# Loading x in 512-byte runs and turning it on VectorE in a quantized feed-forward kernel

## The chip, the cores and the metric
One NeuronCore of a Trainium2 chip runs the whole kernel. The metric is the device time of one execution in microseconds, the median of several.

## What is computed
`x` is (4, 1024, 512) float32, `cond_512` (4, 256). A relation is formed from x, its mean over the sequence and the condition, and goes through a feed-forward part with activations quantized to uint8 steps and weights to int8 steps; the result is added to x:

```python
fused = concatenate([x, x_mean * ones_L, hidden[:, None, :] * ones_L], axis=-1)   # hidden = [cond, cond]
relation = relu(einsum('bld,do->blo', fused, W) + b)          # W (1536, 512)
h = relu(quant_linear(relation, w1, b1))                       # w1 (2048, 512)
out = x + quant_linear(h, w2, b2)                              # w2 (512, 2048)
# quant_linear: s = max(x)/255, xq = clip(round(x/s), 0, 255)*s; each weight row by max|w|/127; bias to s_in*s_w
```

The scale of the activations is the maximum over the whole tensor, so no activation can be quantized before every relation is known.

## The kernel before
The 4096 rows of x are eight blocks n = 0..7 of 512 rows. Five instruction streams are written out by hand and joined by semaphores: SP issues the DMAs, PE is TensorE, ACT ScalarE, DVE VectorE, POOL GpSimd.

**Phase 1, the relation.** The contraction over the depth (512, in KD = 4 chunks of 128) needs x with the depth on the partitions. A block arrives in `x_in` with four consecutive rows of x in each partition (runs of 8 KB; block 0 in two halves with runs of 4 KB, L219). `turn_x` (L332) turns it on TensorE: 16 transposes of 128x128 into the four PSUM banks `XT[k]` (L337; for block 0 L367). ScalarE copies each bank, rounded to float32r, into `x_hi` (`take_hi`, L511) and sums it for the mean; VectorE puts the rest into `x_lo` (`take_lo`, L632). The weight is split in the same manner into `cw_hi` (L543) and `cw_lo` (L670). `relation(n, par, ot)` (L341 to L351) forms one of four tiles of 128 output columns as 12 products of 512 columns, x_hi cw_hi + x_lo cw_hi + x_hi cw_lo for each chunk, in one of two banks `REL`; a tile's bank is free again when `take_relation` (L635, VectorE) has copied it to `raw` with its maximum, which is why `relation` waits for `rel_taken`, two tiles back.

Beside it the weights of the feed-forward part are quantized, one chunk of 1 MB per block: VectorE finds the row maxima (`scale_w`, L642 to L654), ScalarE rounds (L519), VectorE casts (`cast_w`, L659), TensorE transposes (`turn_w`, L353 to L360, 16 transposes), ScalarE copies out (L526, L533).

The order on each engine in block n (x two blocks deep, `par` the buffer): TensorE relation 0, `turn_x(n + 1)`, relations 1 to 3, `turn_w(n)`. VectorE (`phase1_block`, L690): `take_relation(n, 0)`, `scale_w(n)`, `take_lo(n + 1)` for chunks 0 to 2, `take_relation(n, 1)`, `take_lo` for chunk 3, `take_relation(n, 2)`, `cast_w(n)`, `take_relation(n, 3)`. ScalarE: `take_hi(n + 1)`, the rounding of the weights, the copies out. SP: when `x_turned` shows that block n has been read out of x_in, x of block n + 2; when the weights of n have been rounded, the weights of n + 2; after the first two of these, `cw_rest` (the other 1024 rows of W, 2 MB, L247) and `b2_b` (L248). Ahead of block 0 TensorE runs products on the identity (`keep_warm`, L330). Small rows (condition, biases) are turned on TensorE after block 0's x (L375 to L377) and copied by VectorE (L681 to L688).

**Phases 2 and 3.** `product1` (L443) forms the hidden activations, `take_h` (L784) copies them with their maxima, half of them go to DRAM and back; `product2` (L473) forms the output, `finish` (L836) scales it, adds x (`x_res`, loaded again at L270 and L297, 8 KB per partition) and SP stores it (L286, L305).

## Time and profile before

| | us |
|---|---|
| three runs | 355.8, 356.89, 454.16 |
| median | 356.89 |
| span of the profiled execution, first to last instruction | 353.6 |
| TensorE busy in it | 346.3 |
| VectorE busy | 270.5 |
| ScalarE busy | 170.7 |

The profile is of one execution, whose own time is its span; what lies around the span is the difference to the runs. In the rows, PE is TensorE's products, PEld its weight loads, SPq the queue of SP. The names of tensors are those that share the memory: `bank` is PSUM, `hidden` is also `raw`, `pool_r` also cw_in, cw_rest and the weight steps, `pool_q` the raw feed-forward weights. The chain of waits is the work that ended last, followed back; in it and in the timelines a product's end is modelled.

### The profile page before, as it was taken

How to read it: one execution, taken by the hardware profiler on the slowest of the kernel's cores; microseconds unless marked ns; L12 is line 12 of the kernel's file. 1: busy time of each engine (PE TensorE's matmuls, PEld its weight loads, DVE VectorE, ACT ScalarE, POOL GpSimd, SP SyncE). 2: the span in 40 equal slices, each digit the busy share in tenths (PEclk: the TensorE clock that was granted, in tenths of full speed). 3: DMA queues.
4: the chain of work that ended last, by engine and by line, in shares of the span. 5: the costliest groups of instructions: out<-in, count | busy, mean ns of one | idle time of the engine just before them, and what ended most of it. 6: DMA issues, size and time to landing. Idle time of an engine off the chain costs nothing.

```text
span 353.6 us, 5697 instructions
## 1 busy us (share of the span) xinstructions
PE 346.3 (98%) x1774; PEld 202.6 (57%) x1774; DVE 270.5 (77%) x588; ACT 170.7 (48%) x285; POOL 1.1 (0%) x8
## 2 busy tenths in 40 slices
PE   6899999999999999999999999999999999999996
PEld 6688888888887744444444444444444444444444
DVE  1867567576485579999999999988495685785996
ACT  3655546447345299991000000009959569578800
POOL 1000000000000000000000000000000000000000
PEclk9999999999999999999999999999999999999999
DMA  7961981641300007887785030026986279977416
GB/s 265 399 255 43 339 336 59 237 154 83 120 0 2 0 1 294 346 342 326 311 297 224 0 119 0 0 78 244 387 362 237 120 284 424 399 222 222 167 63 237
DMA packets 13295, 70.72 MB, mean 200 GB/s; under 512 B 1224, under 2 KB 1504, under 8 KB 5856
## 3 DMA queue, kind: packets, MB, share of 16 engines
q1 hardware_dynamic: 13280, 70.54, 51.6%
q8 instruction: 8, 0.13, 0.2%
q14 instruction: 7, 0.06, 0.0%
HBM read 45.37 MB, written 25.17 MB: 199 GB/s over the span
## 4 chain that ended last, share of the span: by engine, by line
PE 92%; issue 3%; DVE 3%; DMA 1%; ACT 0%; DVEq 0%
PE bank L480 27%; PE bank L446 26%; PE bank L349 24%; PE bank L501 4%; PE bank L337 3%; PE bank L456 2%; PE bank L359 2%; PE bank L330 1%; DMA x_in<-in_x_dram 1%; DVE hidden L792 1%; PE bank L367 1%; DVE x_lo L632 1%; PE bank L401 1%; PE bank L435 0%; DVE cw_lo L670 0%
## 5 line engine op out<-in xcount | busy, mean ns | idle before, releaser
L592 ACT ACTIVATE steps<-hidden,s_quant 128x512 int16 (+1 forms) x124 | 76.8, 708 | 98.8 <-DVE s_quant L815 78.2
L446 PE MATMUL bank<-pool_r,w_t 128*128 (+1 forms) x480 | 103.8, 379 | 0.0
L792 DVE TENSOR_SCALAR_CACHE_REDUCE hidden<-bank,qb,hmax 128x512 f32 x128 | 97.6, 810 | 6.2 <-PE bank L456 2.3
L446 PEld LDWEIGHTS bank<-pool_r,w_t 128*128 128x128 bf16 x480 | 47.0, 98 | 56.6
L480 PE MATMUL bank<-w_t 128*128 128x512 bf16 x256 | 55.9, 379 | 0.0
L349 PE MATMUL bank<-x_hi,cw_hi 128*128 128x512 f32 x128 | 51.6, 403 | 0.9 <-issue 0.5
L349 PE MATMUL bank<-x_hi,cw_lo 128*128 128x512 f32 x128 | 50.0, 391 | 0.0
L349 PE MATMUL bank<-x_lo,cw_hi 128*128 128x512 f32 x128 | 49.9, 390 | 0.0
L637 DVE TENSOR_SCALAR_CACHE_REDUCE hidden<-bank 128x512 f32 (+1 forms) x32 | 22.0, 689 | 36.1 <-PE bank L349 36.1
L480 PEld LDWEIGHTS bank<-w_t 128*128 128x128 bf16 x256 | 25.0, 98 | 30.2 <-issue 0.2
L480 PE MATMUL bank<-w_t,pool_q 128*128 128x512 bf16 x192 | 41.9, 379 | 0.0
L480 PEld LDWEIGHTS bank<-w_t,pool_q 128*128 128x128 bf16 x192 | 18.8, 98 | 22.6
L349 PEld LDWEIGHTS bank<-x_hi,cw_hi 128*128 128x128 f32 x128 | 24.0, 188 | 7.0 <-issue 1.5
L349 PEld LDWEIGHTS bank<-x_hi,cw_lo 128*128 128x128 f32 x128 | 24.0, 188 | 5.2
L349 PEld LDWEIGHTS bank<-x_lo,cw_hi 128*128 128x128 f32 x128 | 24.1, 188 | 4.5
L511 ACT ACTIVATE x_hi<-bank 128x512 fp32r<-128x512 f32 x32 | 18.7, 598 | 13.7 <-PE bank L337 12.5
L519 ACT ACTIVATE pool_r<-pool_q,winv 128x512 int8<-128x512 f32 x32 | 20.5, 711 | 5.6 <-DVE winv L654 5.6
L632 DVE TENSOR_TENSOR x_lo<-bank,x_hi 128x512 fp32r<-128x512 f32 x32 | 20.6, 682 | 1.1 <-ACT x_hi L511 1.1
L574 ACT ACTIVATE steps<-hidden,bias_inv,s_in_inv 128x512 uint8 (+1 forms) x28 | 20.5, 802 | 1.2 <-ACT pool_r L579 1.2
L823 DVE TENSOR_SCALAR pool_q<-steps 128x2048 bf16<-128x2048 int16 x16 | 10.7, 690 | 13.0 <-ACT steps L592 12.6
L823 DVE TENSOR_SCALAR w_t<-steps 128x2048 bf16<-128x2048 int16 x15 | 10.1, 691 | 12.9 <-ACT steps L592 12.5
L533 ACT ACTIVATE w_t<-bank 128x1024 bf16<-128x1024 bf16 x8 | 7.8, 1020 | 22.7 <-PE bank L359 22.7
(104 smaller groups left out, 268.3 us busy)
## 6 DMA issues: line engine op xcount, KB each, us to landing
hidden_spill<-hidden SPq DMA_DIRECT2D x16, 1024.0 KB, 3.9
hidden<-hidden_spill SPq DMA_DIRECT2D x16, 1024.0 KB, 8.3
pool_q<-in_L_ffn_w_dram SPq DMA_DIRECT2D x8, 1024.0 KB, 5.1
pool_r<-in_x_dram SPq DMA_DIRECT2D x8, 1024.0 KB, 5.7
x_in<-in_x_dram SPq DMA_DIRECT2D x7, 1024.0 KB, 7.1
out_dram<-pool_r SPq DMA_DIRECT2D x7, 1024.0 KB, 6.0
pool_r<-in_L_cond_W_dram SPq DMA_DIRECT2D x1, 2048.0 KB, 10.9
x_in<-in_x_dram SPq DMA_DIRECT2D x2, 512.0 KB, 5.1
```

The lines of the kernel that those rows point to most:

```text
L349: mm = pe.matmul(REL[ot % 2][:, :], w[:, k, ot * P:(ot + 1) * P], v[:, par, k, :], start=(k == 0 and m == 0), stop=(k == KD - 1 and m == 2))
L446: mm = pe.matmul(bank[ft % BANKS][:, :], w1_t[:, k, ft * P:(ft + 1) * P], act_q[:, bass.ds(n * (KD * TB) + k * TB, TB)], start=(k == 0), s ...
L480: mm = pe.matmul(bank[TJ * par + j][:, :], hid_q[par][:, ft, j * P:(j + 1) * P], w2_t[:, ft, :], start=(ft == 0), stop=(ft == FT - 1))
L501: mm = pe.matmul(y_bank[:, cols], hid_q[1][:, ft, j * P:(j + 1) * P], w2_t[:, ft, cols], start=(ft == 0), stop=(ft == FT - 1))
L511: act.activation(x_hi[:, par, k, :], XT[k][:, :], ACT.Copy, accum_out=xsum[:, bass.ds(n * KD + k, 1)]).then_inc(hi_ready, 1)
L519: act.activation(w_steps[:, j * D:(j + 1) * D], w_in[:, par, j * D:(j + 1) * D], ACT.Copy, scale=winv[:, par, s:s + 1]).then_inc(w_steps_r ...
L574: ins = act.activation(act_steps[:, k * TB:(k + 1) * TB], raw[:, bass.ds((n * KD + k) * TB, TB)], ACT.Identity, scale=s_in_inv[:, 0:1], bi ...
L592: ins = act.activation(steps[:, q % 2, f, :], hidden[:, bass.ds(slot * HB + ft * TB, TB)], ACT.Copy, scale=s_quant[:, ft:ft + 1])
L632: dve.tensor_tensor(x_lo[:, par, k, :], XT[k][:, :], x_hi[:, par, k, :].bitcast(F32), ALU.subtract).then_inc(lo_ready, 1)
L637: dve.tensor_scalar(raw[:, bass.ds((n * KD + ot) * TB, TB)], REL[ot % 2][:, :], 1.0, None, ALU.mult, ALU.max, accum_out=raw_max[:, bass.ds ...
L792: dve.tensor_scalar(hidden[:, bass.ds(slot * HB + ft * TB, TB)], bank[ft % BANKS][:, :], qb1[:, ft:ft + 1], hmax[:, ft:ft + 1], ALU.add, A ...
L823: dve.tensor_scalar(hid_q[par][:, 4 * q:4 * q + 4, :], steps[:, q % 2, :, :], 0.0, 255.0, ALU.max, ALU.min).then_inc(hid_ready, 1)
```

## The change
A partition group c (32 partitions) now receives columns 128c to 128c + 127 of x: row 32q + i of the block goes to partition 32c + i, at place q, in runs of 512 bytes, by four DMAs of 32 partitions. VectorE turns each chunk k with one `dve.transpose` of 128x512 (16 squares of 32x32 per group) straight into `XT[k]`. The depth that comes to partition 32c + r of chunk k is 128c + 32k + r, so the weight is loaded in the same order (`cw_turned`), the first 512 rows by eight DMAs on ACT's queue, the next 512 by four on SP's. Block 0's relation runs chunk by chunk of the depth over four banks (`relation_by_depth`), so that it can start with the first chunk. Relations 0 and 1 of block 1 come ahead of `turn_w(0)`, and the small rows are turned behind them. The residual x and the output now go in runs of 2 KB, with row 128j + p in partition p.

```diff
+    R = 32; CG = P // R; TQ = TB // R
+    x_blocks  = ... .rearrange("(n j p) d -> n p j d", p=P, j=TJ)        # was "(n p j) d -> n p (j d)"; out_blocks alike
+    x_squares = ... .rearrange("(n q i) (c e) -> n c i q e", q=TQ, i=R, c=CG)
+    cw_turned = cond_w.rearrange("(g c k r) o -> g c r k o", c=CG, k=KD, r=R)
 # SP
             def load_x(n, par):
-                sp.dma_start(x_in[:, par, :, :]..., x_blocks[...]).then_inc(x_landed[par], 16)
+                for c in range(CG):
+                    sp.dma_start(x_in[c * R:(c + 1) * R, par, :].rearrange("i (q e) -> i q e", q=TQ),
+                                 x_squares[bass.ds(n, 1), c, :, :, :]...).then_inc(x_landed[par], 16)
-            load_half(0, x0_landed); load_cw(range(KD // 2)); load_half(1, x_landed[0])
+            load_x(0, 0)
 ...
-            load_cw(range(KD // 2, KD))
             load_x(1, 1)
 ...
-            sp.dma_start(cw_rest, cw_rows[:, KD:3 * KD, :]).then_inc(rest_landed, 16)
+            for c in range(CG):
+                sp.dma_start(cw_rest[c * R:(c + 1) * R, 0:KD, :], cw_turned[1, c]).then_inc(rest_landed, 16)
+            sp.dma_start(cw_rest[:, KD:KC, :], cw_rows[:, 2 * KD:3 * KD, :]).then_inc(rest_landed, 16)
 # TensorE
-            def turn_x(n, it, par): ...                    # and block 0's transposes
+            def relation_by_depth():
+                for k in range(KD):
+                    pe.wait_ge(lo_ready, k + 1)
+                    pe.wait_ge(cw_lo_ready, k + 1)
+                    for ot in range(KD):
+                        for m, (w, v) in enumerate(((cw_hi, x_hi), (cw_hi, x_lo), (cw_lo, x_hi))):
+                            mm = pe.matmul(bank[4 + ot][:, :], w[:, k, ot * P:(ot + 1) * P], v[:, 0, k, :], ...)
+                        if k == KD - 1:
+                            mm.then_inc(rel_done, 1)
+            keep_warm(50, ident_bf[:, :], REL[0])          # was 20 and 9
+            relation_by_depth()
+            for ot in range(2):
+                relation(1, 1, ot, taken=ot + 1)
+            turn_columns()                                 # waits rows_landed, rel_taken >= KD
+            turn_w(0, 0); turn_w(0, 1)
+            for ot in range(2, KD):
+                relation(1, 1, ot)
+            turn_w(1, 0); turn_w(1, 1)
                 # blocks 2 to 6: relations 0 to 3, turn_w
 # ACT
+            for h in range(2):
+                for c in range(CG):
+                    act.dma_start(cw_in[c * R:(c + 1) * R, ks, :], cw_turned[0, c, :, ks, :]).then_inc(cw_landed[h], 16)
             def take_cw(k):
-                act.wait_ge(cw_landed[k], 16)
+                act.wait_ge(cw_landed[k // 2], 16 * CG)
 # VectorE
+            def turn_x(n, it, par, chunks=range(KD)):
+                dve.wait_ge(x_landed[par], 16 * CG * (it + 1))
+                squares = x_in[:, par, :].rearrange("p (q k r) -> p k q r", q=TQ, k=KD)
+                for k in chunks:
+                    if n > 0:
+                        dve.wait_ge(lo_ready, KD * (n - 1) + k + 1)
+                    dve.transpose(XT[k][:, :].rearrange("p (q i) -> p q i", i=R), squares[:, k, :, :]
+                                  ).then_inc(x_turned, 1)
-            for k in range(KD // 2): take_cw_lo(k)
-            take_lo(0, 0, range(KD // 2))
-            for k in range(KD // 2, KD): take_cw_lo(k); take_lo(0, 0, [k])
+            turn_x(0, 0, 0, [0, 1])
+            for k in range(KD):
+                take_cw_lo(k)
+                take_lo(0, 0, [k])
+                if k + 2 < KD:
+                    turn_x(0, 0, 0, [k + 2])
             def phase1_block(...):
+                elif first:                                # block 0
+                    turn_x(1, 0, 1)
+                    scale_w(n, it, par, w2_rows)
+                    take_lo(1, 1, range(KD - 1))
+                    take_relation(0, 0)
                 else:
+                    turn_x(n + 1, it + par, 1 - par)
                     take_relation(n, 0)
+                    if columns:                            # block 1
+                        take_columns()
                     scale_w(n, it, par, w2_rows)
                     take_lo(n + 1, 1 - par, range(KD - 1))
-            with dve.Fori(0, KD // 2) as it: ...
+            for n in range(KD): phase1_block(n, n // 2, n % 2, False, False, first=(n == 0), columns=(n == 1))
```

## Rows read from the trace of the kernel before

**Rows 1.** The page: busy time of each engine (us, share, instructions).
```profile
PE 346.3 (98%) x1774; PEld 202.6 (57%) x1774; DVE 270.5 (77%) x588; ACT 170.7 (48%) x285; POOL 1.1 (0%) x8
```

**Rows 2.** Chain of waits in order of time: start us, us, what.
```profile
24.78 2.82 PE bank L349 x12
27.61 1.75 PE bank L337 x16
29.35 8.18 PE bank L349 x36
37.53 0.91 PE bank L359 x16
38.44 2.82 PE bank L349 x12
...
120.75 0.71 DVE hidden L637 x2
```

**Rows 3.** Stages: length; busy us of PE, PEld, DVE, ACT, POOL; clock, DMA, GB/s.
```profile
0.00:2.00 2.00, 0.09 (x2) 0.09 (x3) 0.32 (x3) 1.13 (x1) 1.09 (x8) 1.00 0.08 25
2.00:5.00 3.00, 2.22 (x20) 1.96 (x20) 0.00 (x0) 0.16 (x1) 0.00 (x0) 1.00 0.92 231
5.00:7.00 2.00, 1.82 (x9) 1.76 (x10) 0.27 (x1) 0.96 (x2) 0.00 (x0) 1.00 1.02 395
7.00:9.00 2.00, 2.00 (x18) 1.70 (x16) 1.09 (x2) 0.81 (x3) 0.00 (x0) 1.00 1.08 426
...
38.24:51.90 13.66, 13.66 (x85) 11.50 (x82) 8.88 (x18) 7.04 (x17) 0.00 (x0) 1.00 0.89 332
```

**Rows 4.** Timeline of VectorE, block 2: start us, us, what, [idle before it].
```profile
41.47 0.69 DVE L637 TENSOR_SCALAR_CACHE_REDUCE hidden<-bank 128x512 f32 x1 [3.04 <-PE bank L349]
...
42.09 2.28 DVE L646 TENSOR_REDUCE wmax<-pool_q 128x4 f32<-128x2048 f32 x1
...
44.87 1.89 DVE L632 TENSOR_TENSOR x_lo<-bank,x_hi 128x512 fp32r<-128x512 f32 x3
46.67 0.68 DVE L637 TENSOR_SCALAR_CACHE_REDUCE hidden<-bank 128x512 f32 x1
...
47.28 0.69 DVE L632 TENSOR_TENSOR x_lo<-bank,x_hi 128x512 fp32r<-128x512 f32 x1
```

**Rows 5.** Timeline of the start, TensorE, ACT and VectorE in turn; last, line L763.
```profile
1.91 2.31 PE L330 MATMUL bank<-ident_bf 128*128 128x128 bf16 x20 [1.91 <-POOL ident_bf L318]
...
5.99 1.31 ACT L543 ACTIVATE cw_hi<-pool_r 128x512 fp32r<-128x512 f32 x2 [3.83 <-DMA pool_r<-in_L_cond_W_dram]
...
10.41 0.68 DVE L670 TENSOR_TENSOR cw_lo<-pool_r,cw_hi 128x512 fp32r<-128x512 f32 x1
...
12.81 0.17 DVE L681 TENSOR_REDUCE fold<-ident 128x4 f32<-128x16 f32 x1
...
13.81 0.17 DVE L688 COPY b_col<-bank 128x16 f32<-128x16 f32 x1
...
L763 DVE TENSOR_SCALAR pool_r<-steps x4: 294/294/295, 123.9 to 126.4; 128x512 bf16<-128x512 int16 x4
```

**Rows 6.** Busy time by stretch at the end of the run, columns as in rows 3.
```profile
350.00:351.00 1.00, 0.30 (x3) 0.02 (x1) 0.63 (x2) 0.00 (x0) 0.00 (x0) 1.00 0.93 272
...
352.00:353.00 1.00, 0.00 (x0) 0.00 (x0) 0.00 (x0) 0.00 (x0) 0.00 (x0) 0.90 0.37 131
353.00:353.60 0.60, 0.00 (x0) 0.00 (x0) 0.00 (x0) 0.00 (x0) 0.00 (x0) 0.50 0.00 0
```

**Rows 7.** SP timeline, x_in issues; DMA issues with median us to landing.
```profile
20.75 0.50 SPq L202 DMA_DIRECT2D x_in<-in_x_dram  x1
...
35.85 0.56 SPq L202 DMA_DIRECT2D x_in<-in_x_dram  x1
...
pool_q<-in_L_ffn_w_dram SPq DMA_DIRECT2D x8, 1024.0 KB, 5.1
...
x_in<-in_x_dram SPq DMA_DIRECT2D x7, 1024.0 KB, 7.1
```

More of the change, by code:

```diff
@@ L330, in keep_warm, with relation @@
                     pe.matmul(free_bank[:, 0:moving.shape[-1]], ident_bf[:, :], moving, start=True, stop=True)
-            def turn_x(n, it, par):
-                pe.wait_ge(x_landed[par], 16 * (it + 1))
-                for k in range(KD):
-                    pe.wait_ge(lo_ready, KD * (n - 1) + k + 1)
-                    for j in range(TJ):
-                        mm = pe.transpose(XT[k][:, j * P:(j + 1) * P], x_in[:, par, j, k * P:(k + 1) * P],
-                                          ident[:, :])
-                    mm.then_inc(x_turned, 1)
-            def relation(n, par, ot):
-                pe.wait_ge(rel_taken, KD * n + ot + 1)
+            def relation(n, par, ot, taken=None):
+                pe.wait_ge(rel_taken, KD * n + ot - 1 if taken is None else taken)
                 for k in range(KD):
@@ L379, in _ @@
+            keep_warm(50, ident_bf[:, :], REL[0])
[3 more added lines that the diff above has]
+            turn_columns()
+            for half in range(2):
+                turn_w(0, half)
+            for ot in range(2, KD):
+                relation(1, 1, ot)
+            for half in range(2):
+                turn_w(1, half)
+            with pe.Fori(1, NB // 2 - 1) as it:
                 for par in range(2):
                     n = 2 * it + par
-                    relation(n, par, 0)
@@ L382, in _ @@
-                    turn_x(n + 1, it + par, 1 - par)
-                    for ot in range(1, KD):
+                    for ot in range(KD):
                         relation(n, par, ot)
@@ L388, in _ @@
             n = NB - 2
-            relation(n, 0, 0)
-            turn_x(n + 1, NB // 2 - 1, 1)
-            for ot in range(1, KD):
+            for ot in range(KD):
                 relation(n, 0, ot)
@@ L733, in _ @@
             by_batch = raw_max[:, :].rearrange("p (b h k) -> p h b k", h=2, k=KD)
-            with dve.Fori(0, KD // 2) as it:
-                for par in range(2):
-                    phase1_block(2 * it + par, it, par, False, False)
+            for n in range(KD):
+                phase1_block(n, n // 2, n % 2, False, False, first=(n == 0), columns=(n == 1))
             for n in range(KD, NB - 1):
```

124 lines of the change are left out of this document (53 added, 71 removed).

## The prediction

> **What bounds the kernel now.** I read the busy shares first. TensorE is busy for 346.3 of 353.6 us, VectorE for 270.5 [rows 1], so a microsecond is gained only where TensorE stops working, and VectorE isn't free either. Next the chain of waits in order of time [rows 2]: after the first 15 us it is TensorE alone through the first phase, and each 512-row block repeats four pieces: 36 products of the relation (8.18 us, so 0.227 us a product), 16 transposes of weights (0.91), 12 products (2.82), 16 transposes of x on L337 (1.75). From 24.78 to 38.44 is one block: 13.66 us. The last relation is taken at 120.75; the two later phases begin from there and hold none of the changed instructions except transfers. The table by stage then shows the room [rows 3]: in one such block VectorE works 8.88 of 13.66 us. Its own timeline [rows 4] shows where the room lies: one idle stretch of 3.04 us ahead of `take_relation(n, 0)`; between `take_relation(n, 0)` at 41.47 and the end of `take_relation(n, 1)` at 47.28 there is none.
>
> **What goes from TensorE.** Seven groups of 16 transposes (L337) of 1.75 us, 12.3 us, and those of block 0 (L367). If nothing took their place, six blocks would give 10 us and more.
>
> **What comes to VectorE.** 32 `dve.transpose` of 128x512 float32 in 16 squares each, SBUF to PSUM. No row shows one. From below: a 128x512 operation that only clips and converts, 0.29 us (L763). From above: each of the 16 squares paid like the smallest copy, 0.17 us (L688), 16 x 0.17 = 2.7 us [rows 5]. The nearest rows are the subtractions of the same size and type, which start 0.60 us apart when nothing holds them (four from 10.41 to 12.81) [rows 5]. I take 0.61, since a transpose reads and writes as many elements. Call it T.
>
> **Steady blocks (2 to 6).** Four T's stand between `take_relation(n-1, 3)` and `take_relation(n, 0)`, in the gap of 3.04 us [rows 4]. VectorE waits there for the transposes of weights and the first 12 products, and not for the x transposes, which came behind these; so the gap stays, and 4 x 0.61 = 2.44 us fit. They fit up to T = 0.77. What shows up is another wait. The fourth relation of a block may not start before `take_relation(n, 1)` has freed its bank. In the old order TensorE had 1.75 us of x transposes plus two relations (2 x 12 x 0.227 = 5.45 us) between the first and the fourth; now it has 5.45 alone. VectorE needs, from the end of the first relation (38.44 + 2.82 = 41.26 [rows 2]), 0.21 until it starts, 5.81 until 47.28, and some 0.08 for the semaphore: 6.10, against a start of the fourth at 5.45 less 0.16 (a product's end is modelled that much after its slot) = 5.29. So TensorE stalls 0.8 us per block. A block costs 13.66 - 1.75 + 0.80 = 12.7 us. Five blocks gain 5 x 0.95 = 4.75 us.
>
> **Start.** Here VectorE becomes the bound. x(0) now needs all 1 MB (four transfers) before the first transpose, with 1 MB of the weight on ACT's queue beside it. The old rates were 25 GB/s to 2 us, 231 to 5, 395 to 7, 426 to 9 [rows 3]; 2.1 MB are through at 8.4. The first cw_hi started at 5.99 [rows 5], 0.8 us after its bytes (0.79 MB into the queue) by these rates: so x(0) at 9.2 if runs of 512 bytes move as those of 4 KB. No row has such runs; if they move at half the rate (one row already shows 231 instead of 395), 11.9; if x goes ahead of the weight, 7. I take 10.0.
>
> From there VectorE has, without a pause, up to the release of relation (1, 3): 12 transposes (x(0), x(1), x(2)) 7.3 us; 15 subtractions (cw_lo 4, x_lo 4+4+3) at 0.60, 9.0; six relations taken at 0.62 (46.67 to 47.28), 3.7; two `scale_w` at 2.78 (42.09 to 44.87), 5.6; one cast 1.1; `take_columns` 1.2 (12.81 to 13.98) [rows 4, 5]. Sum 27.9 us, so the fourth relation of block 1 starts at 38.0 and the transposes of W(1) at 38.0 + 2.73 + 0.16 = 40.9. Before they stood at 37.53 [rows 2]. The start loses 3.4 us, though the relation of block 0 by depth keeps TensorE fed from the first chunk (first product about 12.6, last about 23.5): it stands still some 1.6 us ahead of block 1 and some 3 us ahead of relation (1, 3).
>
> **The clock.** TensorE now has a gap, from the end of 50 warm products (20 took 2.31 us [rows 5], so 1.9 + 5.8 = 7.7) to 12.6. At the end of the run the granted clock is 1.00 until 352, with the last products at 350.3, 0.90 in the next microsecond and 0.50 (1.2 GHz) behind it [rows 6]. So I expect the first products of block 0 at 1.2 GHz. Cover: relation (0, 0) ends some 2.5 us before VectorE comes to take it, so a loss up to 2.5 us costs nothing. The Trainium skill ("TensorE: Matmul & The Clock Gate", part 1) says that an idle array falls to half clock; the trace agrees, and with the cover the sum is the same unless the low clock stays, the rival below.
>
> **Transfers.** Later x loads are issued two blocks ahead (20.75, 35.85) and take a median of 7.1 us [rows 7]; four issues in place of one cost SP some 1.2 us (0.50 to 0.56 for one [rows 7], less where little waits), behind which only the next load waits. ACT now issues eight loads of the weight first, 8 x 0.45 = 3.6 us, and x_hi isn't wanted before 10.6: hidden. The tight one is x(4): it stands in SP's queue behind w(3), the 2 MB of cw_rest and b2 (it was issued at 35.85 before [rows 7]). w(3) now waits until about 41; 4.5 MB at 395 GB/s are 11.3 us, plus 0.9, so x(4) lands at about 54.2 and VectorE wants it at 54.7. VectorE waits in `turn_x`, and behind it stand `take_relation(3, 0)`, then `scale_w`, so TensorE would follow. I add 0.6 us for what that may miss (bounds 0 and 3). The stores and residual loads in runs of 2 KB instead of 8 KB (phase 3) have the w1 loads as a pattern: 5.1 us per 1 MB with 2 KB and 8 KB rows together [rows 7]; chunks are needed tens of microseconds after issue: nothing. The unrolled loops of VectorE: nothing, or a few tenths.
>
> **Sum.** +3.4 - 4.75 + 0.6 = -0.75 us: a span of 352.9. Of the three runs 454.16 lies far off and is left aside; 355.8 and 356.89 lie 2.2 to 3.3 above the profiled span of 353.6. That makes 355.1 to 356.2; I say 355.7. A measurement of this kernel tells about 2% (7.1 us) from no change.
>
> **Rivals.**
> *A, chance 0.59:* the above. Its bounds: T 0.55 to 0.75, x(0) at 8 to 12: -3.5 to +3, so 353 to 359.5.
> *B, the transposes cost more than the gap hides (slower), 0.15.* Each T above 0.61 costs 12 times its excess in the start, and above 0.77 also 4 x 5 times in the blocks, after which VectorE bounds the phase. T = 1.0: 4.7 + 4.6 - 0.75 = +8.5, 364; T = 1.2: 7.1 + 8.6 - 0.75 = +15, 371. 2% is passed from T = 0.95. For it: 16 separate squares, float32, a destination in PSUM; no row shows any of them. Against: three operations of 512 float32 elements (subtraction, taking a relation, a quarter of the reduction of 2048 in 2.28 us) all cost 0.57 to 0.62 in a row [rows 4, 5].
> *C, the loads at half rate, 0.13.* x(0) comes at 11.9, +1.9; one MB at half of 395 GB/s costs 2.65 us more, so x(4) comes 2.1 us after it is wanted, 1.5 more than I have added: +3.4 in all, 359.1. If the weight's loads on 32 partitions halve too, 1.3 to 2.65 more: up to 362. The Trainium skill ("SBUF — State Buffer", the DMA port swizzle) says that 32 partitions reach only 8 of the 16 ports, and ("DMA: Bandwidth & Descriptors", rules for authors) that splitting over partitions brings nothing; no row of before has a bulk load of 32 partitions, so whether it holds here is open. By that rule the result is C's.
> *D, faster by over 2%, 0.06.* T near 0.3 (-3.8 in the start) and x(0) at 7 (-3), beside my -0.75: -7.5, 349. Only the start can give this much; the stall of 0.8 per block remains whatever T is. Against: both ends needed at once.
> *E, the low clock stays through block 0, 0.07.* 48 products at 0.45: +10.9 less 2.5 covered: +8.4, 364. Against: once it runs, TensorE has 12 products per chunk without a pause.
>
> Numbers: faster 0.07 (D and a trace of A), slower 0.18 (B's larger part and E), the same 0.75. The range 351 to 362 leaves out B and E's larger part above and D below.
>
> **What would show it.** Right: `dve.transpose` at 0.60 to 0.70; blocks 2 to 6 at 12.7 us, with TensorE idle 0.8 us in each ahead of the fourth relation, released by `take_relation(n, 1)`; VectorE without idle time from x(0)'s landing to about 40 us; W(1) at about 41. Wrong: a transpose over 0.8 us; blocks of 11.9 us (no stall); VectorE waiting for x_in in any block; a clock of 0.50 beyond the first chunk; phases 2 and 3 longer than before.

## The result and the profile after

The changed kernel is slower: four runs from 363.68 to 365.58 us, median 364.46. The four runs of the kernel before are 355.53, 355.8, 356.89 and 454.16 (median 356.35); the last lies far off, and the ratio, 1.0242 with a 95% interval of 1.0213 to 1.0272, is taken without it. The profiled execution took 363.68 us with a span of 361.9 us, so the span has grown by 8.3 us, where the prediction had it shrink by 0.75. All of it lies in phase 1: from the last relation taken to the end of the span it was 232.85 us before (353.6 less 120.75 [rows 2]) and is 232.67 after (361.9 less 129.23).

The page of the kernel after, with what answers to [rows 1]; the row of L645 is the new transpose on VectorE (count | busy us, mean ns of one | idle us ahead of it):

```profile
span 361.9 us, 5473 instructions
PE 337.2 (93%) x1645; PEld 192.7 (53%) x1667; DVE 288.7 (80%) x620; ACT 170.2 (47%) x285; POOL 1.1 (0%) x8
...
L645 DVE STREAM_TRANSPOSE bank<-x_in 128x512 f32<-128x512 f32 x32 | 20.2, 694 | 18.5 <-DMA x_in<-in_x_dram 18.5
```

TensorE is busy 9.1 us less (346.3 to 337.2; more than that went in transposes, but more warm products and products at a low clock, below, count in it), and yet the end is later, so TensorE now stands idle for 24.7 us instead of 7.3. The page also says where to look: ahead of the transposes VectorE waited 18.5 us for loads of x.

The waits of the kernel after (us in total, times, longest) cut this into two pieces:

```profile
DVE bank L645 <- DMA x_in<-in_x_dram: 18.5, 2, 10.8
...
PEld bank L338 <- DVE hidden L651: 11.7, 7, 5.6
```

Two waits: 10.8 us is the start, the other 7.75 us comes later. The second row is TensorE's wait for a bank of a relation; seven times, the longest 5.6 us. The chain of waits in order of time (start us, us, what) puts them in place; beside [rows 2]:

```profile
2.24 9.80 DMA x_in<-in_x_dram
...
14.61 13.32 PE bank L358 x48
...
47.47 1.88 SPq L210
49.53 4.75 SPq L210
54.47 10.57 DMA x_in<-in_x_dram
65.06 2.50 DVE bank L645 x4
...
68.20 8.38 PE bank L338 x24
...
129.23 0.71 DVE hidden L651 x2
```

The transposes of weights (L359 before, L348 after, 16 in a row) mark each block, since they stand behind its last relation. Call them W(n). To compare like with like I take all of them from TensorE's timeline; the chain of waits, which models the ends of products, puts them up to 0.16 us later (37.53 for 37.37 [rows 2]). First W(1) and W(6) of the kernel before, 13.65 us per block apart:

```profile
37.37 1.07 PE L359 MATMUL bank<-ident_bf,pool_r 128*128 128x128 bf16 x16
...
105.64 1.07 PE L359 MATMUL bank<-ident_bf,pool_r 128*128 128x128 bf16 x16
```

Then W(1) to W(4) and W(6) after, with two stalls:

```profile
43.80 1.07 PE L348 MATMUL bank<-ident_bf,pool_r 128*128 128x128 bf16 x16
...
53.53 0.50 PE L338 MATMUL bank<-x_hi,cw_hi 128*128 128x512 f32 x1 [0.42 <-DVE hidden L651]
...
56.41 1.07 PE L348 MATMUL bank<-ident_bf,pool_r 128*128 128x128 bf16 x16
...
68.20 0.79 PE L338 MATMUL bank<-x_hi,cw_hi 128*128 128x512 f32 x1 [5.19 <-DVE hidden L651]
68.80 0.63 PE L338 MATMUL bank<-x_lo,cw_hi 128*128 128x512 f32 x1
69.22 0.63 PE L338 MATMUL bank<-x_hi,cw_lo 128*128 128x512 f32 x1
...
76.42 1.07 PE L348 MATMUL bank<-ident_bf,pool_r 128*128 128x128 bf16 x16
...
88.99 1.07 PE L348 MATMUL bank<-ident_bf,pool_r 128*128 128x128 bf16 x16
...
114.12 1.07 PE L348 MATMUL bank<-ident_bf,pool_r 128*128 128x128 bf16 x16
```

So three terms make up the loss up to W(6), 114.12 - 105.64 = 8.48 us:

| | before | after | difference | predicted |
|---|---|---|---|---|
| W(1) | 37.37 | 43.80 | +6.4 | +3.4 |
| blocks 2, 4, 5, 6, each | 13.65 | 12.56 to 12.61 | -1.04 to -1.09, four: -4.3 | -0.95 |
| block 3 | 13.65 | 20.01 | +6.4 | -0.95 + 0.6 |

Block 3 (counted from W(2) to W(3)) is where x(4) comes late. VectorE's own timeline shows both landings and the size of the transpose (start us, us, line and operation, count, idle time ahead and its releaser):

```profile
12.06 1.32 DVE L645 STREAM_TRANSPOSE bank<-x_in 128x512 f32<-128x512 f32 x2 [10.76 <-DMA x_in<-in_x_dram]
...
19.25 2.48 DVE L645 STREAM_TRANSPOSE bank<-x_in 128x512 f32<-128x512 f32 x4
21.65 2.24 DVE L659 TENSOR_REDUCE wmax<-pool_q 128x4 f32<-128x2048 f32 x1
...
38.35 1.89 DVE L636 TENSOR_TENSOR x_lo<-bank,x_hi 128x512 fp32r<-128x512 f32 x3 [0.89 <-ACT x_hi L512]
...
65.06 2.50 DVE L645 STREAM_TRANSPOSE bank<-x_in 128x512 f32<-128x512 f32 x4 [7.75 <-DMA x_in<-in_x_dram]
...
73.13 0.08 DVE L651 DVE_READ_ACCUMULATOR hidden<-bank 128x1 f32 x1
```

Four transposes take from 19.25 to 21.65, 0.60 us each: the predicted price (0.61). x(0) can be read at 12.06 instead of 10.0, and x(4) at 65.06 instead of 54.2. The last row is the end of `take_relation(3, 1)`, to which the part on the clock comes back.

Why the loads are late, the table by stage shows (columns as in [rows 3]; the clock, the DMA share and GB/s stand last):

```profile
5.00:7.00 2.00, 1.58 (x23) 1.41 (x21) 0.00 (x0) 1.02 (x1) 0.00 (x0) 1.00 1.18 202
7.00:9.00 2.00, 0.00 (x0) 0.00 (x0) 0.00 (x0) 0.00 (x0) 0.00 (x0) 0.98 1.14 188
9.00:11.00 2.00, 0.00 (x0) 0.00 (x0) 0.00 (x0) 0.32 (x1) 0.00 (x0) 0.50 1.12 255
...
17.00:20.00 3.00, 3.00 (x10) 2.37 (x9) 3.00 (x6) 0.69 (x2) 0.00 (x0) 0.64 1.05 333
20.00:24.00 4.00, 4.00 (x19) 3.27 (x18) 3.96 (x5) 2.46 (x8) 0.00 (x0) 1.00 1.08 342
```

From 5 to 9 us the loads move 188 to 202 GB/s where before they moved 395 and 426 [rows 3], and the DMA share is 1.14 to 1.18: the queues are full, only the bytes are few. Of TensorE's clock the same rows show that it was granted at 1.00 (2.4 GHz) while the warm products ran, that it stood at 0.50 (1.2 GHz) after TensorE had stopped, and that it was back at 1.00 by 20 us. It fell once more in block 3, behind the stall of 5.19 us: the products from 68.20 on start 0.42 to 0.43 us apart, where at 2.4 GHz they start 0.23 apart, and the granted clock is 0.50 from 68 to 73 us.

### The profile page after: what moved, and what is told of

Its sections match the earlier page's. It is cut to its first block, busy times and chain, and to the rows that moved or that the text cites. A ratio compares the mean times of both kernels' runs of the same rounds, so it can differ in the third digit from the quotient of the medians.

```text
span 361.9 us, 5473 instructions
## 1 busy us (share of the span) xinstructions
PE 337.2 (93%) x1645; PEld 192.7 (53%) x1667; DVE 288.7 (80%) x620; ACT 170.2 (47%) x285; POOL 1.1 (0%) x8
## 3 DMA queue, kind: packets, MB, share of 16 engines
q10 hardware_dynamic: 640, 1.05, 1.3%
## 4 chain that ended last, share of the span: by engine, by line
PE 77%; DVE 8%; DMA 6%; issue 4%; SPq 3%; ACT 1%; ACTq 0%; DVEq 0%
PE bank L481 27%; PE bank L447 25%; PE bank L338 12%; DMA x_in<-in_x_dram 6%; PE bank L502 4%; PE bank L358 4%; SPq L210 2%; PE bank L457 2%; DVE wmax L659 2%; DVE x_lo L636 2%; DVE hidden L651 1%; PE bank L348 1%; DVE hidden L809 1%; PE bank L328 1%; DVE bank L645 1%
## 5 line engine op out<-in xcount | busy, mean ns | idle before, releaser
L338 PE MATMUL bank<-x_hi,cw_hi 128*128 128x512 f32 x112 | 46.3, 413 | 8.9 <-DVE hidden L651 8.9
L338 PE MATMUL bank<-x_hi,cw_lo 128*128 128x512 f32 x112 | 44.7, 399 | 0.0
L338 PE MATMUL bank<-x_lo,cw_hi 128*128 128x512 f32 x112 | 44.6, 399 | 0.0
L645 DVE STREAM_TRANSPOSE bank<-x_in 128x512 f32<-128x512 f32 x32 | 20.2, 694 | 18.5 <-DMA x_in<-in_x_dram 18.5
L651 DVE TENSOR_SCALAR_CACHE_REDUCE hidden<-bank 128x512 f32<-128x512 f32 x32 | 21.8, 685 | 13.1 <-PE bank L338 13.1
L338 PEld LDWEIGHTS bank<-x_hi,cw_hi 128*128 128x128 f32 x112 | 21.6, 193 | 16.7 <-DVE hidden L651 11.7
L338 PEld LDWEIGHTS bank<-x_hi,cw_lo 128*128 128x128 f32 x112 | 21.6, 193 | 4.8
L338 PEld LDWEIGHTS bank<-x_lo,cw_hi 128*128 128x128 f32 x112 | 21.8, 195 | 4.1
L840 DVE TENSOR_SCALAR pool_q<-steps 128x2048 bf16<-128x2048 int16 x16 | 10.7, 690 | 12.9 <-ACT steps L596 12.6
```

The source lines that it names most:

```text
L338: mm = pe.matmul(REL[ot % 2][:, :], w[:, k, ot * P:(ot + 1) * P], v[:, par, k, :], start=(k == 0 and m == 0), stop=(k == KD - 1 and m == 2))
L645: dve.transpose(XT[k][:, :].rearrange("p (q i) -> p q i", i=R), squares[:, k, :, :]).then_inc(x_turned, 1)
L651: dve.tensor_scalar(raw[:, bass.ds((n * KD + ot) * TB, TB)], y_bank[:, :], 1.0, None, ALU.mult, ALU.max, accum_out=raw_max[:, bass.ds(n * ...
L840: dve.tensor_scalar(hid_q[par][:, 4 * q:4 * q + 4, :], steps[:, q % 2, :, :], 0.0, 255.0, ALU.max, ALU.min).then_inc(hid_ready, 1)
```

## Experiments

W(n) keeps its meaning in all of them. Ratios are to the kernel before, run on the same chip. A single run has no interval. Where an edit adds lines, line numbers are shifted by a few.

**1. The second stall: what stands ahead of x(4).** The loads of the second part of the weight and of b2 are issued after all other loads of phase 1.

```diff
             # SP, after blocks 0 and 1
-            for c in range(CG):
-                sp.dma_start(cw_rest[c * R:(c + 1) * R, 0:KD, :], cw_turned[1, c]).then_inc(rest_landed, 16)
-            sp.dma_start(cw_rest[:, KD:KC, :], cw_rows[:, 2 * KD:3 * KD, :]).then_inc(rest_landed, 16)
-            sp.dma_start(b2_b[:, :], b2.partition_broadcast(P)).then_inc(b2_landed, 16)
             with sp.Fori(1, 3) as it:
                 ...
+            # the same four statements here
```

> The changed kernel with the loads of cw_rest and b2 (2.25 MB) moved in SP's order from ahead of x(4) to behind the last load of x and of the weights; everything is still computed. Theory Q (x(4) comes late because 2.25 MB stand ahead of it in the queue, in a stage in which x itself moves slowly): VectorE's wait of 7.75 us ahead of block 4's transposes shrinks to under 1 us, and the span falls from 361.9 by about 7 to 355. Theory I (SP's own issue of the x loads, 8.9 us for four, is what delays x(4), whatever stands ahead): the wait stays above 4 us and the span falls by less than 3.

Measured: 357.3 us (357.02 to 357.75), ratio 1.0041 (1.0026 to 1.0055), span 356.0. The wait ahead of block 4's transposes is gone; VectorE waits for x once, at the start:

```profile
DVE bank L646 <- DMA x_in<-in_x_dram: 11.8, 1, 11.8
```

W(1) stands at 45.21 and the five blocks behind it take 12.6 us each up to 108.19. The span is 5.9 us shorter, although the start was later here (x(0) at 13.08, W(1) 1.4 us behind that of the changed kernel); so x(4), standing behind 2.3 MB that nobody needs before the end of phase 1 (TensorE uses them at 115.19 in the chain of after), had cost some 7.3 us. What is left is the start, 7.8 us late here, less some 5.3 that the five blocks give.

**2. What makes the loads slow: the length of the runs or the number of partitions.** Four kernels hold the new order of work and all its instructions on the engines, and change only the kind of loads. Other elements of x (and in the fourth of W) arrive, so none of them computes the reference; the amount of work is the same. First x in runs of 512 bytes, but each load to all 128 partitions:

```diff
-    x_squares = ... .rearrange("(n q i) (c e) -> n c i q e", q=TQ, i=R, c=CG)
+    x_pieces = ... .rearrange("(n p j) (c e) -> n c p j e", p=P, j=TJ, c=CG)
 ...
-                    sp.dma_start(x_in[c * R:(c + 1) * R, par, :].rearrange("i (q e) -> i q e", q=TQ), x_squares[...]
+                    sp.dma_start(x_in[:, par, c * TB:(c + 1) * TB].rearrange("p (j e) -> p j e", j=TJ), x_pieces[...]
```

> The changed kernel, but each of the four loads of an x block goes to all 128 partitions, 4 runs of 512 bytes each, instead of to 32 partitions with 16 runs (the data that arrive are other elements of x, so the output isn't the reference's; the amount of work is the same). Theory R (runs of 512 bytes are what is slow): first transpose at about 12 us, wait ahead of block 4 still about 7 us, span about 362. Theory P (32 partitions at a time are what is slow): first transpose at about 9.5, wait ahead of block 4 under 2 us, span about 354.

Then the other trait alone, 32 partitions with runs of 8 KB:

```diff
+    x_rows = ... .rearrange("(n c i j) d -> n c i (j d)", c=CG, i=R, j=TJ)
 ...
+                    sp.dma_start(x_in[c * R:(c + 1) * R, par, :], x_rows[...]
```

> The changed kernel, but each of the four loads of an x block brings rows in runs of 8 KB to its 32 partitions (other elements of x arrive, so the output isn't the reference's; the amount of work is the same). Theory R (runs of 512 bytes are slow): first transpose at about 9.5 us, wait ahead of block 4 under 2 us, SP's issues of x(4) under 3 us in all, span about 353. Theory P (32 partitions at a time are slow): first transpose at about 12, wait about 7 us, span about 362.

Then neither, 128 partitions with runs of 2 KB, for x alone (the weight still by 32 partitions):

```diff
+    x_pieces = ... .rearrange("(n p j) d -> n j p d", p=P, j=TJ)
 ...
+                    sp.dma_start(x_in[:, par, c * TB:(c + 1) * TB], x_pieces[...]
```

> The changed kernel with each x load over all 128 partitions in runs of 2 KB (other elements of x arrive, so the output isn't the reference's; the amount of work is the same), so neither of the two suspected traits is left in the x loads; the weight's loads on 32 partitions stay. If run length and partitions explain the loss together: x moves at 380 to 400 GB/s, first transpose at about 9.3 us, no wait ahead of block 4 above 2 us, span 353 to 355. If something else of the change holds it back (issue by SP, the weight's loads): first transpose later than 11 or a wait above 4.

Measured, in one run each, so that the timelines say more than the totals: 512 bytes over 128 partitions 360.66 us (span 358.9), 8 KB on 32 partitions 365.92 (364.1), 2 KB over 128 partitions 357.9 (356.1). None of the three met its expectation in full: neither theory alone holds, and without either trait in x the wait ahead of block 4 was still 3.61 us, with `cw_rest` unchanged in front of it. The views of the DMA queues from 10 to 40 us, 40 slices of 0.75 us in GB/s, show the rates themselves. Each holds a stretch of 380 to 390 which is the two first chunks of the feed-forward weights (128 partitions, unchanged; 2.1 MB, some seven slices), and x(1) and x(2) stand on its two sides, x(1) beside what is left of the narrow weight loads. The kernel after, with that stretch from the twelfth slice:

```profile
GB/s 247 252 230 212 186 173 214 189 178 197 287 388 388 393 385 382 388 285 183 183 176 216 197 161 119 266 388 382 374 236 187 182 193 198 181 130 46 0 0 0
```

512 bytes over 128 partitions, the stretch from the eighth slice:

```profile
GB/s 217 201 213 293 291 290 309 365 388 385 385 385 390 369 330 294 290 291 208 15 0 0 11 117 330 401 412 299 292 308 320 270 36 11 0 11 0 0 0 0
```

8 KB on 32 partitions, the stretch again from the twelfth:

```profile
GB/s 262 161 221 205 238 221 238 218 131 218 295 382 382 388 388 388 434 251 208 175 197 240 229 0 11 0 0 90 197 418 385 391 300 229 197 251 197 153 0 11
```

2 KB over 128 partitions, where it goes on from the sixth slice for eleven, because x(2) behind it runs at the same rate:

```profile
GB/s 238 268 273 295 265 361 391 385 388 391 391 390 380 377 391 391 347 123 3 0 0 0 85 161 355 415 401 216 199 350 393 189 44 0 0 11 0 0 0 0
```

So x moves mostly at 176 to 216 with both traits, at about 290 with the short runs alone, at about 200 to 240 on 32 partitions alone, and at 390 with neither. The partitions are the larger cause, the runs of 512 bytes a second one, and together they are not much worse than the partitions alone. The first transpose follows (12.06, 11.02, 10.09, 10.80 us), with the weight's loads sharing the queues in each; so does the wait ahead of block 4's transposes (7.75, 4.22, 8.22, 3.61 us). In the kernel with 8 KB on 32 partitions x(0) was early but the weight late: VectorE waited 3.87 us for `cw_hi` at 19.09. In that with 512 bytes over 128 partitions the clock added to the loss: TensorE had waited twice for some 2 us in block 3, its clock was at 0.50 from 70 to 72 us, and the last relation of the block took 4.46 us (68.90 to W(3) at 73.36) where it takes 2.9 at full clock.

The runs of 512 bytes cost something else, on SP. The four issues of x(4) in the kernel after and in that with 8 KB on 32 partitions, from SP's timeline:

```profile
42.52 0.38 SPq L222 DMA_DIRECT2D pool_q<-in_L_ffn_w_dram  x1
...
46.94 8.91 SPq L210 DMA_DIRECT2D x_in<-in_x_dram  x4
56.05 3.17 SPq L222 DMA_DIRECT2D pool_q<-in_L_ffn_w_dram  x1
```

```profile
48.53 1.88 SPq L210 DMA_DIRECT2D x_in<-in_x_dram  x4
```

8.91 against 1.88 us for the same four issues (8.96 with 512 bytes over 128 partitions). The chain of waits above runs through these issues, but that they made x(4) late is not borne out: with 1.88 us x(4) came later still (67.39, its issue having begun 1.6 us later).

**3. All loads of the kind of before.** The fourth kernel takes both traits from all loads: x as in the last, both parts of the weight in the rows and sizes of the kernel before. The order of the loads, `cw_rest` ahead of x(4) included, stays that of the change.

```diff
+                    sp.dma_start(x_in[:, par, c * TB:(c + 1) * TB], x_pieces[...]
 ...
-            for c in range(CG):
-                sp.dma_start(cw_rest[c * R:(c + 1) * R, 0:KD, :], cw_turned[1, c]).then_inc(rest_landed, 16)
-            sp.dma_start(cw_rest[:, KD:KC, :], cw_rows[:, 2 * KD:3 * KD, :]).then_inc(rest_landed, 16)
+            sp.dma_start(cw_rest, cw_rows[:, KD:3 * KD, :]).then_inc(rest_landed, 16)
 ...
-            for h in range(2):
-                for c in range(CG):
-                    act.dma_start(cw_in[c * R:(c + 1) * R, ks, :], cw_turned[0, c, :, ks, :]).then_inc(cw_landed[h], 16)
+            for k in range(KD):
+                act.dma_start(cw_in[:, k, :], cw_rows[:, k, :]).then_inc(cw_landed[k // 2], 16)
```

> The kernel of e8_wide2k with the weight's loads over all 128 partitions too (cw_in by four loads in runs of 2 KB, cw_rest by one as in the kernel before); other elements of x and W arrive, so the output isn't the reference's. Now no load differs in kind from those of the kernel before, while the transposes on VectorE, the new order and the order in SP's queue are those of the changed kernel. If the kind of the loads is what the prediction missed: first transpose at 8.5 to 9.3 us, wait ahead of block 4 under 1.5 us, and the span as predicted, 352 to 354. If the order of the queue by itself makes x(4) late: a wait of 3 us or more and a span of 355 or more.

Measured: 355.01 us (354.09 to 356.12, ten runs), ratio 0.9979 (0.9963 to 0.9995), span 353.4. From VectorE's timeline, the landings of x(0) and x(4):

```profile
9.84 1.32 DVE L640 STREAM_TRANSPOSE bank<-x_in 128x512 f32<-128x512 f32 x2 [8.54 <-DMA x_in<-in_x_dram]
...
56.76 2.51 DVE L640 STREAM_TRANSPOSE bank<-x_in 128x512 f32<-128x512 f32 x4 [1.56 <-DMA x_in<-in_x_dram]
```

W(1) is at 41.68, W(6) at 105.64, and the last relation is taken at 120.75, to the hundredth where it was before. This is the experiment that settles the case: the ratio to the kernel before is 0.9979 here and 1.0242 for the changed kernel, and nothing but the loads differs, their kind and with it the number of issues (the weight in five instead of thirteen). Of the 8.5 us of span, 2.12 are W(1) and 6.4 block 3 (13.57 instead of 20.01), in which the wait for x(4) fell from 7.75 to 1.56.

**4. The cause put into the kernel before.** If 32 partitions are the cause, they must cost there too. Each load of x is split into four of 32 partitions, runs of 8 KB and 4 KB kept; nothing else changes.

```diff
             # kernel before
-                sp.dma_start(x_in[:, par, :, :]..., x_blocks[...]).then_inc(x_landed[par], 16)
+                for c in range(4):
+                    ps = slice(c * 32, (c + 1) * 32)
+                    sp.dma_start(x_in[ps, par, :, :]..., x_blocks[bass.ds(n, 1), ps, :]...).then_inc(x_landed[par], 16)
```

> The kernel before with TensorE's transposes and its 8 KB runs, but every x load split into four of 32 partitions each: the one trait of the new loads alone, everything still computed. Theory P (loads of 32 partitions at a time move at about half the rate, whoever transposes): x alone moves at 200 to 240 GB/s instead of 390 to 400; block 0's second half and x(1) land later, and the span grows by 2 to 5 us at the start; from block 2 on blocks stay at 13.66 us. Theory N (it is the combination with the short runs or with VectorE's transposes): rate of x above 350 GB/s and the span within 1 us of 353.6.

Measured: 358.85 us (358.14 to 360.05), ratio 1.0072 (1.005 to 1.0093), span 358.3. Table by stage of the kernel before, then of this one:

```profile
4.00:12.00 8.00, 6.38 (x39) 5.08 (x37) 4.16 (x7) 4.72 (x12) 0.00 (x0) 1.00 1.01 383
12.00:17.00 5.00, 4.76 (x29) 3.84 (x29) 4.46 (x10) 2.42 (x8) 0.00 (x0) 1.00 1.07 406
```

```profile
4.00:12.00 8.00, 4.77 (x28) 4.17 (x25) 1.56 (x3) 2.16 (x5) 0.00 (x0) 1.00 1.02 238
12.00:17.00 5.00, 5.00 (x16) 3.82 (x15) 4.32 (x11) 2.56 (x8) 0.00 (x0) 1.00 1.01 198
```

The same loads in the same order: 383 becomes 238 and 406 becomes 198 GB/s, with the DMA share about as full (1.02 and 1.01). In the profiled execution, the longest of the four, the last relation is taken at 125.34 instead of 120.75, and all of it is the start (the transposes of block 0's weights, in the chain at 23.87 before, are at 28.47); the blocks stay at 13.65 us: here a load is issued two blocks ahead.

**5. Both halves of the partitions at once.** If a load of 32 partitions leaves part of the transfer path idle, two loads to different halves of the partitions, from two queues, should use more of it. SP loads partitions 0 to 63, ACT 64 to 127, of x and of the first part of the weight; runs of 512 bytes, as in the change, and `cw_rest` where the change has it.

```diff
             # SP
-                for c in range(CG):
+                for c in range(CG // 2):
                     sp.dma_start(x_in[c * R:(c + 1) * R, par, :]..., x_squares[...]).then_inc(x_landed[par], 16)
             # ACT
+            def load_x_high(n, par):
+                for c in range(CG // 2, CG):
+                    act.dma_start(x_in[c * R:(c + 1) * R, par, :]..., x_squares[...]).then_inc(x_landed[par], 16)
             # the weight's first part likewise: groups 0, 1 on SP, 2, 3 on ACT
```

> The changed kernel, but of the four x loads of each block two (partitions 0 to 63) are issued by SP and two (64 to 127) by ACT, so that both halves of the partitions are written at once; the weight's loads for block 0 are split over the two queues in the same way, behind x(0). Order and size of the rest stay, cw_rest and b2 too. Theory P (loads that write only some partitions at a time get half the rate): while x alone is loaded the rate rises from about 185 GB/s towards the 290 of runs of 512 bytes over all partitions; the first transpose comes at 8 to 9.5 us instead of 12.1; VectorE's wait ahead of block 4 falls from 7.75 to under 5; the span falls from 361.9 to 353 to 357. Theory R (the run length alone sets the rate): first transpose at 11 or later, rate below 200 GB/s, span above 360.

Measured: 360.17 us (359.61 to 361.71), ratio 1.0123 (1.0105 to 1.0141), span 359.9.

```profile
7.79 1.32 DVE L662 STREAM_TRANSPOSE bank<-x_in 128x512 f32<-128x512 f32 x2 [6.50 <-DMA x_in<-in_x_dram]
...
62.84 2.51 DVE L662 STREAM_TRANSPOSE bank<-x_in 128x512 f32<-128x512 f32 x4 [7.79 <-DMA x_in<-in_x_dram]
```

By stages of 2 us the loads move 320, 287 and 299 GB/s from 8 to 14 us (225, 243 and 201 in the kernel after), and x(0) is readable at 7.79 instead of 12.06, 4.3 us sooner. Those 4.3 us are not all rate: on both queues x(0) now stands ahead of the weight, where in the changed kernel the two came beside each other, and from 5 to 7 us the loads moved 222 GB/s against 202. What x(0) gains, the weight does not: VectorE then waits 1.30 us for `cw_hi`, and W(1) at 41.56 is 2.2 us sooner. The rates from 8 us on still show that two loads of 32 partitions beside each other do better than one behind the other. Which part of that is the second queue and which the other half of the partitions this kernel does not tell. The expectation for the rest was missed: the span is 359.9 and not 353 to 357, since x(4) still stood behind the narrow `cw_rest`, on SP's queue, and VectorE waited for it as long as before (7.79 us).

**6. The low clock at the start.** 128 warm products instead of 50, meant to keep TensorE at work until shortly before its first relation.

```diff
-            keep_warm(50, ident_bf[:, :], REL[0])
+            keep_warm(128, ident_bf[:, :], REL[0])
```

> The changed kernel with 128 warm products instead of 50, at 0.093 us each, so that TensorE works from 1.9 to about 13.9 us and block 0's relation begins at 2.4 GHz. The prediction's step (the low clock in block 0 is hidden behind VectorE): block 0's 48 products take 10.9 us instead of 13.3, TensorE waits 2.4 us longer ahead of block 1, and the span stays within 0.4 us of 361.9. Theory W (the low clock costs its 2.4 us): the span falls by 2 us or more.

Measured: 362.89 us (361.95 to 365.49), ratio 1.0221 (1.0174 to 1.0267), span 360.4. The edit did only part of what it was meant to do. The first six products of block 0 come at 2.4 GHz, 0.23 us apart, but the warm products were over 3.60 us before them, and from 16.3 to about 19.3 us the products are 0.43 apart again, at a granted clock of 0.50:

```profile
14.69 0.50 PE L358 MATMUL bank<-x_hi,cw_hi 128*128 128x512 f32 x1 [3.60 <-DVE x_lo L636]
15.03 0.40 PE L358 MATMUL bank<-x_lo,cw_hi 128*128 128x512 f32 x1
15.26 0.40 PE L358 MATMUL bank<-x_hi,cw_lo 128*128 128x512 f32 x1
```

The 48 products take 12.6 us instead of 13.3, and not the 10.9 expected. So this run tests only a small part of the low clock: from the transposes of x(1) to W(1) it is 24.33 us here (19.97 to 44.30) and 24.55 in the kernel after (19.25 to 43.80). The better evidence is the kernel after itself. From 12.06 to 33.25 us VectorE, which bounds the start, waits for nobody; then it waits 0.47 us for the small rows from TensorE, and TensorE waits 2.1 us for VectorE ahead of relation (1, 3). The low clock at the start cost half a microsecond at most. The 1.5 us by which this span is shorter come from the wait for x(4), 5.97 us here and 7.75 there; why x(4) came sooner is not shown.

**7. The stall in every block.** TensorE's wait ahead of the fourth relation (0.42 us in the rows above) should follow from `take_relation(n, 1)`, which comes behind three `x_lo`. Here, in the kernel of experiment 1, it comes ahead of all four.

```diff
-                    take_lo(n + 1, 1 - par, range(KD - 1))
                 take_relation(n, 1)
-                if not last:
-                    take_lo(n + 1, 1 - par, [KD - 1])
+                if not last and not first:
+                    take_lo(n + 1, 1 - par, range(KD))
+                if first:
+                    take_lo(1, 1, [KD - 1])
```

> The kernel of e1_rest_late, and in blocks 1 to 6 VectorE takes the second relation ahead of the four x_lo subtractions instead of behind the first three. Theory S (the step of the prediction: in a steady block TensorE stands still because the fourth relation waits for take_relation(n, 1)): the gap of about 0.7 us ahead of the fourth relation is gone, blocks 2 to 6 go from 12.6 us to 11.9 to 12.0, and the span falls from 356.0 by 3 to 4 us. Rival V (VectorE as a whole bounds the block, 11.1 of 12.6 us busy): the wait only moves to the first relation or the transposes of weights, blocks stay at 12.5 or more, the span within 1 us.

Measured: 354.85 us (353.93 to 356.97, seven runs), ratio 0.9976 (0.995 to 1.0002); the profiled execution, with a span of 355.0, is one of the longer ones. The waits of TensorE for `take_relation` do not stand in its list of waits any more, and the transposes of x show the length of a block:

```profile
59.33 2.50 DVE L646 STREAM_TRANSPOSE bank<-x_in 128x512 f32<-128x512 f32 x4
71.48 2.50 DVE L646 STREAM_TRANSPOSE bank<-x_in 128x512 f32<-128x512 f32 x4
```

12.15 us in place of 12.6. Four blocks (3 to 6) give 1.9 us; block 2 gives 1.0 back (W(2) at 58.80 against 57.81). The relations of block 1 are over sooner, but the cast of its weights comes no sooner (it starts at 43.79 against 43.92), so TensorE stands still for 2.30 us ahead of W(1), its clock falls to 0.50 from 45 to 48 us, and block 2 takes 13.72 us. Against experiment 1 that leaves 0.9 us at W(6) in the profiles (107.25, 108.19) and 2.4 us in the medians. The stall is real, with about 0.5 us a block; the 3 to 4 us of span that were expected for it did not come.

**8. All repairs together.** Experiments 1, 5 and 7 in one kernel, with 100 warm products.

> e5_early_k1 and e6_two_queues together (late cw_rest and b2, second relation taken early, x over two queues), with 100 warm products. If the three terms add up (7 for x(4), 3.3 for the steady stall, 3 for the start), the span is 361.9 - 13 = 349 and the kernel is faster than both: 350.5 us, ratio to the kernel before 0.985. If the start is bounded by VectorE's work alone and the loads come no earlier, 352 to 353.

Measured: 353.63 us (353.08 to 354.08), ratio 0.9949 (0.9931 to 0.9967), span 351.3, the lowest median here; 349 and 350.5 us were expected if the terms added up. It beats the changed kernel by 10.8 us of median and the kernel before by 2, which is a quarter of what a comparison of 2% would call faster. From VectorE's timeline:

```profile
7.78 1.32 DVE L663 STREAM_TRANSPOSE bank<-x_in 128x512 f32<-128x512 f32 x2 [6.49 <-DMA x_in<-in_x_dram]
...
10.36 0.69 DVE L698 TENSOR_TENSOR cw_lo<-pool_r,cw_hi 128x512 fp32r<-128x512 f32 x1 [1.25 <-ACT cw_hi L563]
...
29.35 2.50 DVE L663 STREAM_TRANSPOSE bank<-x_in 128x512 f32<-128x512 f32 x4 [1.81 <-DMA x_in<-in_x_dram]
```

The terms don't add up to their sum. x(0) is there 4.3 us sooner, but VectorE then waits for the weight (1.25) and for x(2) (1.81), and W(1), at 42.80, is only 1.0 us sooner than in the changed kernel.

**9. One more order of the loads.** In the last kernel the second chunk of the feed-forward weights goes behind x(2), so that x(2) does not wait for it.

```diff
-            load_w(w1_chunks, 1, 1)
 ...
                 load_x(n + 2, n)
+                if n == 0:
+                    load_w(w1_chunks, 1, 1)
```

> The kernel of e7_all with the load of the second chunk of w1 (1 MB) issued behind x(2) instead of ahead of it. In e7_all x(2) was issued at 14.1 us and landed at 29.3, with VectorE waiting 1.81 us. Theory L (the start is still bounded by the order of the loads, since x moves slowly): the wait is gone, and the span falls from 351.3 by 1.3 to 2 us. Theory V (the start is bounded by VectorE's own work and the dependence on the small rows): within 0.5 us of 351.3.

Measured: 354.2 us (352.02 to 356.22), ratio 0.994 (0.9904 to 0.9975), span 353.4. The wait for x(2) is gone, but in this profile x(0) is readable at 8.83 instead of 7.78 and VectorE waits 1.41 us for the first chunk of weights. The runs scatter by 4.2 us, and the interval holds the ratio of the kernel without the edit: no gain that can be told.

## Why the prediction was wrong

**The step that failed is the rate of the loads**, in "I take 10.0" for x(0) and in "4.5 MB at 395 GB/s are 11.3 us" for x(4). I carried the rate of loads to 128 partitions over to loads of 32, for which I had said myself that no row of before has one. Rival C named the mechanism, with a chance of 0.13, and ended at 362, 2.5 us short. Experiment 3 shows that this step alone turned a change of nothing into a loss: with the rate restored the span is 353.4 against 352.9 predicted, and the time 355.0 against 355.7. That it comes so near is in part luck: the start then loses 4.3 us and not 3.4, x(4) costs 1.0 and not 0.6, and the blocks gain 5.3 and not 4.75.

*Start.* x(0) at 12.06: C's 11.9, and not 10.0. W(1) then follows the predicted work of VectorE: predicted 30.9 us behind x(0) (10.0 to 40.9, in the count of the chain), measured 31.7 (12.06 to 43.80, 31.9 in that count) and, with the loads at full rate, 31.8 (9.84 to 41.68). The microsecond too few is in sight: VectorE waited 0.89 us for `x_hi` at 38.35, because ScalarE had first to copy out W(0), and 0.47 us for the small rows, two waits that the sum, "without a pause", did not hold.

*x(4).* The prediction had it land at 54.2; its own terms, 41 + 11.3 + 0.9, give 53.2, and C rests on the same slip. It came at 65.06. Going by the measured rates from 53.2: the chunk ahead of it was issued at 42.52 instead of 41 (+1.5); 2.1 MB of narrow loads (x(4) and half of `cw_rest`) at about 190 instead of 395 GB/s take 11.0 instead of 5.3 us (+5.7); and the chunk of weights issued behind x(4), at 56.05, moved beside it, which the bytes in this stretch suggest (5.6 MB from 42.52 to 65.06 where x(4) and what stands ahead of it are 4.5), 1.05 MB at 390 (+2.7). That is 63.1. Of the 2.0 us left, up to 1.5 can be that the queue was not full at first, a DMA share of 0.65 from 42.5 to 46.9 us; the rest is open. Rival C had counted the first of the two narrow megabytes, the second only as an addition at its upper end, and neither the later issue nor the chunk behind. The bounds for this term (0 and 3 us) were much too near; the measured term was 7.4 (20.01 against 12.57). The mistake behind it: a late load passes to TensorE all but in full once the little slack is used up (7.75 us of wait became 7.4, 3.61 became 3.0, 1.56 became 1.0), and I bounded the effect by the slack that I hoped for, not by the slowest rate times the bytes in the queue.

*What held.* T: 0.61 predicted, 0.60 measured. Blocks: 12.7 predicted, 12.56 to 12.61 measured; the reason was the right one (`take_relation(n, 1)` releases the fourth relation, and experiment 7 takes it away), but it is 0.5 to 0.6 us instead of 0.8 (starts 0.80 us apart where they are 0.23 without a stall; experiment 7 takes 0.5 off a block), and a block without it takes 12.15 instead of the 11.9 of the sum: two errors of opposite sign, of which I can name only the first. The clock at the start: at 1.2 GHz until about 19 us, 48 products in 13.3 us, all but hidden as predicted. ScalarE's issues and phases 2 and 3, stores and residual loads in 2 KB runs among them: nothing (232.85 and 232.67 us). Rivals B, D and E are out: T is 0.60, x(0) came later, and the clock came back.

*What the prediction did not have: the clock behind the stall.* After the 5.19 us of idle time in block 3, twelve products ran at 1.2 GHz, and the block's last 24 products took 8.2 us (68.20 to 76.42) where 24 at 0.23 take 5.5. Little of it shows at the end, because VectorE came late too: `take_relation(3, 1)`, which releases the last relation, was read out at 73.13 and finished 0.08 later, and in block 4 the product behind it starts 0.14 us after the start of that read (86.00 to 86.14). At full clock the last relation would have begun at about 73.3 instead of 73.5, and W(3) have come some 0.3 us sooner. With 512 bytes over 128 partitions nothing hid it, and it cost 1.6 us (experiment 2). A stall of TensorE may thus be paid twice; here VectorE's work covered the second payment.

*The rule weighed against the trace.* Measured first: loads to 32 partitions in series ran at 176 to 240 GB/s and those to 128, in runs of 2 KB or more, at 390. The Trainium skill ("SBUF — State Buffer", the DMA port swizzle) says that a group of 32 partitions reaches 8 of the 16 ports; by that rule a series of such loads runs at half rate, and the trace agrees. No row of before spoke against the rule; such a load had only never been made there. An unopposed rule deserved more than 0.13, and its price the whole queue.

**Open.** Why four issues take 8.91 us of SP with runs of 512 bytes and 1.88 with 8 KB when the queue is full is not shown. How the gain of experiment 5 divides between two queues, two halves and the order of x(0) and the weight was not tried, nor x(0) ahead of the weight with everything else as in the change. Nor was a layout whose loads reach all 128 partitions and still bring each square where VectorE's transposes want it.

## What to carry to other kernels

A new layout that makes an engine's work cheaper must be priced at the loads that feed it: how many partitions each load reaches and how long its runs are decide its rate, and where no row of the profile has that kind of load, its cost is the largest unknown of the sum, to be bounded by the bytes in the queue over the slowest rate that can be defended. When a load becomes slower, look down its queue for the next load that has a deadline, and put what nobody needs yet behind it: here one move of four statements brought back 5.9 us of 8.3. Gains in steady blocks are easy to predict and small; one late load in one block outweighs five of them.

## What the runs showed that was not expected

- 32 transposes on VectorE of 128x512 float32 from SBUF to PSUM cost 0.60 us each in a row, as much as a subtraction of that size.
- x moved at 390 GB/s over 128 partitions with runs of 2 KB, at about 290 with runs of 512 bytes, at about 200 to 240 on 32 partitions with 8 KB, at 176 to 216 on 32 partitions with 512 bytes. The DMA share was 1.0 to 1.2 while the slow loads moved (1.14 to 1.18 at 188 to 202 GB/s in the kernel after, 1.01 at 198 in experiment 4), so the busy share of the queues does not show the loss; only the bytes do.
- Two queues, each with loads of 32 partitions of its own half, reached 287 to 320 GB/s from 8 to 14 us with the same runs of 512 bytes, where one queue moved 201 to 243.
- SP took 8.91 us for four issues with runs of 512 bytes in a full queue, and 1.88 us with 8 KB. The chain of waits runs through them, but x(4) came no sooner with the short issues, so what they cost is not shown.
- TensorE's clock fell to 0.50 behind a stall in mid-kernel, at 68 us in the kernel after and at 45 us in experiment 7, and the 12 products behind the first of these started 0.42 to 0.43 us apart instead of 0.23.
